# Adding eight gathered expert rows to each token: eight multiply-and-add operations against one wide product, one sum and one addition

## The chip, the cores and the metric

The kernel runs on one core of one Trainium2 chip. The metric is the device time of one execution in microseconds (us); lower is better. The engines of the core are PE (TensorE, the matrix engine; PEld is its weight load), DVE (VectorE), ACT (ScalarE), POOL (GpSimd) and SP (SyncE, which here only issues transfers). A [P, 128] tile holds 128 tokens on 128 partitions and 128 features in the free dimension, float32.

## What is computed

4096 tokens of 128 features pass through two layers, each an attention and a mixture of experts with residual additions:

```
x = x + tanh(g_xattn[0]) * attention0(layernorm(x), ctx)
x = x + tanh(g_ffn[0])   * mixture0(layernorm(x))      # 64 experts, 8 for each token, 2 shared
x = x + tanh(g_xattn[1]) * attention1(layernorm(x), ctx)
x = x + tanh(g_ffn[1])   * mixture1(layernorm(x))      # 8 experts, 2 for each token
```

The part that matters here is the end of mixture0. The router gives each token eight experts with a weight each, `rw`, and

```
routed = einsum('eth,te->th', expert_out, rw)
```

so that eight rows of 128 numbers, each times its token's weight (the gate tanh(g_ffn[0]) is already in it), are added to the token's row of `x`.

## The kernel before

Tokens are held as 32 tiles of 128 (TILES), in two halves of 16 (HTILES); 16 groups of two tiles (GROUPS) go through the attention, each engine running a loop of steps j in which up to six groups are in flight at different stages. There is no scheduler: every engine has its own instruction list, written out by hand, and waits on semaphores. An instruction that waits holds all that stand behind it on its engine.

Mixture0 works by expert. POOL scatters the normalised rows to their experts' places in DRAM (L1794). Then 112 blocks n of work run, 16 for the shared experts and 96 (RTB, index m = n - 16) for the routed ones, four tiles of 128 rows in each. In each block PE turns the rows and multiplies by the gate and up weights (L830), ACT applies the activation (L1092), DVE multiplies the two parts (`hidden`, L1579), PE turns the product and DVE copies it out of PSUM (`copy_hidden`, L1587), PE multiplies by the down weights (L856), ACT copies the results and they are stored to `expert_results` in DRAM (L1100).

The way back is: POOL issues one indirect DMA for each tile t and rank k (`gather`, L1813), which fetches for every token its k-th row; 256 of them in all. They fill a ring: four buffers for the first 16 tiles (`yg`, laid in `xn2T`), seven for the last 16 (`late_rows`, `late_more`). `gathered(t)` gives the buffer, its semaphore and the count at which all eight rows are there. A buffer is fetched into again only when its tile has been combined, which POOL waits for on the semaphore `s_comb` (L1806 and after). The first half's gathers start about when the second half's routed blocks are under way.

DVE combines: `combine_part(t, part)` takes two of the eight ranks, with one SCALAR_TENSOR_TENSOR each (x = rows[:, k] * wk[:, k] + x, L1710), each waiting for the one before through `s_comb`. PIECES is 4. Tiles 0 to 10 (SOONER is 11) are combined in the routed blocks, one part in each block from m = COMBINE_AT[t] = HRTB + 7 + t * 11 // 3 on, after that block's `hidden` and `copy_hidden`. After each pair of tiles `late_stats` (L1684, L1688) takes the next layernorm's statistics at m = COMBINE_AT[2g+1] + PIECES; POOL turns them into 1/deviation (`deviation`, L1835 and L1837) at a fixed place in its list of gathers, and DVE's `late_neg` (L1695) follows at + PIECES + 4.

Tiles 11 to 31 are combined by `combine(t)`, all parts in a row, as the last thing of a step j of the second attention (L1494 and L1517). The steps have one or two tiles: 5, 9, 11, 12 and 13 have two, and so has step 1. The next step of DVE begins with `late_stats` and `max_rows` (L1226), the maximum over the scores; PE's `shift` (L615) waits for it. POOL's list in these steps has up to ten gathers, one `late_deviation` and one `deviation2` (again L1835 and L1837), for which DVE's `norm2_neg` (L1275) waits. Later the gathers are followed by the scatter of the second mixture (L1820).

## Time and profile before

| | before |
|---|---|
| median of 3 runs | 1156.08 us (1152.35 to 1157.39) |
| the profiled execution, its own time | 1156.52 us |
| its span, first to last instruction | 1154.7 us |
| mean granted TensorE clock | 0.881 of 2.4 GHz |
| PE busy | 992.8 us (86%) |
| DVE busy | 749.3 us (65%) |
| POOL busy | 697.1 us (60%) |
| the 256 operations on L1710 | 89.0 us of DVE |

Busy shares are means over stages that have different limits, so the stage has to be looked at: 274 to 664 us are the blocks of mixture0, 664 to 945 us the second attention with the gathers and combines in it, and from there on mixture1. A timeline row has start, duration (us), engine, line, operation, output<-input and shapes; in square brackets the idle time before it and what ended it. "issue" means that nothing in the profile shows a reason.

### The profile page before, as it was taken

The numbers are of one execution on the slowest core, as the hardware profiler recorded it, in microseconds if no ns is written. First come the engines' busy times: TensorE is split into PE (matmuls) and PEld (weight loads), VectorE is DVE, ScalarE is ACT, GpSimd is POOL, SyncE is SP. The second block draws the span as 40 slices with busy tenths as digits, with TensorE's granted clock in tenths as the row PEclk, the third lists the DMA queues.
The fourth block names the chain that finished last, engine by engine and source line by source line (L and its number), as shares of the span: only waits on it lengthen the run. The fifth ranks groups of instructions, "written<-read, shape, count | busy, mean of one in ns | idle before, by whom it ended". The sixth has DMA issues, their size and how long they took to land.

```text
span 1154.7 us, 28212 instructions
## 1 busy us (share of the span) xinstructions
PE 992.8 (86%) x8822; PEld 854.9 (74%) x8822; DVE 749.3 (65%) x2773; ACT 609.9 (53%) x1505; POOL 697.1 (60%) x767
## 2 busy tenths in 40 slices
PE   4888888887997799999999948778889998999991
PEld 2566666665786699999999926666677778999991
DVE  4568888875884378786667635478867644534563
ACT  2566666644332355555555435567564555756660
POOL 1105777776777676006777777777766467765542
PEclk9899999987996799999999965799775667999996
DMA  7434622521246677567777653334222113323434
GB/s 201 99 81 111 165 65 86 154 75 40 70 143 185 187 219 215 168 170 211 221 212 220 185 153 87 91 100 109 57 59 59 41 45 92 91 85 83 139 89 128
DMA packets 228050, 144.03 MB, mean 125 GB/s; under 512 B 55058, under 2 KB 213186, under 8 KB 227906
## 3 DMA queue, kind: packets, MB, share of 16 engines
q1 hardware_dynamic: 151618, 65.37, 21.1%
q0 software_dynamic: 20992, 43.30, 12.4%
q10 hardware_dynamic: 55296, 33.56, 10.2%
q8 instruction: 76, 1.25, 0.5%
q14 instruction: 68, 0.56, 0.2%
HBM read 78.76 MB, written 64.49 MB: 124 GB/s over the span
## 4 chain that ended last, share of the span: by engine, by line
PE 45%; POOL 16%; DVE 14%; issue 9%; DMA 8%; SPq 6%; ACT 3%; DVEq 0%; POOLq 0%; ACTq 0%
PE bank L830 6%; DMA expert_results<-arena 6%; PE bank L856 5%; PE bank L905 4%; PE bank L915 4%; POOL late_more L1813 4%; PE bank L639 3%; PE bank L626 3%; POOL expert_rows L1820 3%; PE bank L807 2%; SPq L487 2%; PE bank L604 2%; PE bank L841 2%; DVE x L1710 2%; PE bank L676 2%
## 5 line engine op out<-in xcount | busy, mean ns | idle before, releaser
L1794 POOL DMA_INDIRECT expert_rows<-xn2T,slot x256 | 252.1, 985 | 95.3 <-issue 72.1
L1813 POOL DMA_INDIRECT xn2T<-expert_results,slot x128 | 124.0, 969 | 102.5 <-DMA expert_results<-arena 64.3
L830 PE MATMUL bank<-wexp,arena 128*128 x768 | 144.9, 334 | 2.3 <-issue 1.1
L986 ACT ACTIVATE work<-bank 128x512 f32<-128x512 f32 x128 | 76.6, 599 | 98.3 <-PE bank L626 95.8
L830 PEld LDWEIGHTS bank<-wexp,arena 128*128 128x128 f32 x768 | 120.2, 197 | 8.2 <-issue 6.4
L1579 DVE TENSOR_TENSOR arena<-arena,bank 128x176 f32<-128x176 f32 x224 | 70.1, 334 | 84.6 <-ACT arena L1092 77.2
L1134 ACT ACTIVATE arena<-bank,wcopy 128x128 f32<-128x128 f32 x320 | 90.8, 370 | 53.9 <-PE bank L905 52.9
L1100 ACT ACTIVATE arena<-bank 128x512 f32<-128x512 f32 x96 | 57.3, 597 | 110.6 <-DMA expert_results<-arena 67.7
L1830 POOL DMA_INDIRECT expert_results<-yb,back x80 | 79.6, 995 | 59.1 <-DVE yb L1732 35.8
L856 PE MATMUL bank<-wexp,arena 88*128 x768 | 107.3, 285 | 5.3 <-ACT arena L1100 4.8
L626 PE MATMUL bank<-cst,work 128*128 128x128 f32 x512 | 98.4, 323 | 14.4 <-DVE arena L1241 7.6
L639 PEld LDWEIGHTS bank<-vm,work 128*64 128x64 f32 x2048 | 83.0, 159 | 30.8 <-ACT work L986 20.0
L856 PEld LDWEIGHTS bank<-wexp,arena 88*128 88x128 f32 x768 | 97.7, 199 | 7.8 <-issue 7.4
L1092 ACT ACTIVATE arena<-bank 128x176 f32<-128x176 f32 x224 | 68.6, 317 | 65.5 <-PE bank L830 33.5
L639 PE MATMUL bank<-vm,work 128*64 128x18 f32 x2048 | 96.2, 230 | 4.4 <-ACT work L986 4.1
L1587 DVE COPY arena<-bank 88x512 f32<-88x512 f32 x112 | 76.6, 684 | 29.9 <-PE bank L841 29.5
L1226 DVE TENSOR_REDUCE nmax<-bank 128x8 fp32r<-128x512 f32 x128 | 85.1, 673 | 16.1 <-PE bank L610 10.8
L990 ACT ACTIVATE work<-bank 128x512 f32<-128x512 f32 x128 | 76.3, 596 | 33.8 <-PE bank L615 33.4
L905 PE MATMUL bank<-xgT,wcopy 128*128 128x128 f32 x640 | 88.8, 283 | 4.6 <-DVE wcopy L1725 4.6
L615 PE MATMUL bank<-nmax,idr 128*128 128x512 f32 x128 | 70.2, 549 | 23.2 <-DVE nmax L1226 23.2
L915 PE MATMUL bank<-wx,arena 128*128 x640 | 85.2, 277 | 0.7 <-ACT arena L1134 0.7
L655 PE MATMUL bank<-arena,wqk 128*128 128x256 f32 x192 | 64.5, 450 | 24.4 <-DVE arena L1241 11.4
(211 smaller groups left out, 2148.0 us busy)
## 6 DMA issues: line engine op xcount, KB each, us to landing
arena<-expert_rows SPq DMA_DIRECT2D x384, 64.0 KB
expert_results<-arena ACTq DMA_DIRECT2D x96, 256.0 KB
expert_rows<-zero SPq DMA_DIRECT2D x130, 64.0 KB
arena<-in_ctxT ACTq DMA_DIRECT2D x32, 256.0 KB
xg<-expert_rows SPq DMA_DIRECT2D x80, 68.0 KB
expert_rows<-xn2T,slot POOLq DMA_INDIRECT x320
wx<-in_mix SPq DMA_DIRECT2D x16, 256.0 KB
late_rows<-expert_results SPq DMA_DIRECT2D x8, 512.0 KB
```

Source lines behind the costliest of these rows:

```text
L626: mm = pe.transpose(w[:, bb * P:(bb + 1) * P], work[:, u, bb * P:(bb + 1) * P], ident)
L639: mm = pe.matmul(w2[b2 * SEQ:(b2 + 1) * SEQ, at:at + 2 * VW], work2[:, u % 2, pair * P + b2 * SEQ:pair * P + (b2 + 1) * SEQ], vm[:, V % 3, ...
L830: mm = pe.matmul(out[:, b * 2 * I0:(b + 1) * 2 * I0], xgT[:, n % 2, 2 * h + b, :], wflat[:, bass.ds(offsets[m][2 * h + b], 2 * I0)], start ...
L856: mm = pe.matmul(bank[7][:, b * P:(b + 1) * P], hT[0:I0, n % 2, b, :], wflat[0:I0, bass.ds(offsets[m][b] + 2 * I0, P)], start=True, stop=T ...
L905: mm = pe.matmul(bank[2 + i % 3][:, c * P:(c + 1) * P], wcopy[:, i % WRING, c * P:(c + 1) * P], xgT1[:, m % 2, i % NB, :], start=True, sto ...
L915: mm = pe.matmul(bank[LATE_Y[m % 2]][:, b * P:(b + 1) * P], hT1[:, i % WRING, c, :], wxflat[:, bass.ds(offsets[m][b] + (W2C + c * P), P)], ...
L986: act.activation(work2[:, u % 2, :], (w0, w3, w3, w3)[u][:, :], ACT.Copy).then_inc(S["pt_copied"], 1)
L1134: a = act.activation(hT1[:, i % WRING, c, :], bank[2 + i % 3][:, c * P:(c + 1) * P], ACT.Gelu_apprx_tanh, bias=wcopy[:, i % WRING, F1 + c: ...
L1226: dve.tensor_reduce(nmax[:, u, :], score[u][:].rearrange("p (a k) -> p a k", k=SEQ), AX.X, ALU.max, negate=True).then_inc(S["max_done"], 1)
L1794: pool.indirect_dma_start(xs, bass.IndirectOffsetOnAxis(ap=slot[:, t, k:k + 1], axis=0), xn2all[:, t, :].bitcast(I32), None).then_inc(s_sc ...
L1813: pool.indirect_dma_start(rows[:, k, :].bitcast(I32), None, ys, bass.IndirectOffsetOnAxis(ap=slot[:, t, k:k + 1], axis=0)).then_inc(ready, 16)
L1830: pool.indirect_dma_start(ys1, bass.IndirectOffsetOnAxis(ap=back[:, i:i + 1], axis=0), yb1[:, m % YR, b, :].bitcast(I32), None).then_inc(s ...
```

## The change

`combine_part` no longer does two ranks in a part. With PIECES = 3, part 0 waits for the eight rows and multiplies all of them in place by the eight weights, one TENSOR_TENSOR over 8 x 128 = 1024 elements for each partition with the weight broadcast along the features; part 1 sums the eight rows with one TENSOR_REDUCE that reads them feature by feature (a step of 128 elements, 512 bytes, within a sum) into one of two 128-element buffers of the first router (`masked` and `rest`); part 2 adds these to the token's row. Each still waits for the one before through `s_comb`, which now counts 3 for a tile, and all waits on it are rescaled. The parts of a tile in the blocks end one block sooner, and `late_stats` and `late_neg` move one block sooner with them.

```diff
-PIECES = 4
+PIECES = 3
@@ the same in every wait on s_comb, one of them shown
-                    pool.wait_ge(s_comb, (t - ring + 1) * TOPK0)
+                    pool.wait_ge(s_comb, (t - ring + 1) * PIECES)
@@ combine_part(t, part)
-                dve.wait_ge(ready, count)
-                if t % HTILES == 0:
+                if part == 0:
+                    dve.wait_ge(ready, count)
+                if part == 0 and t % HTILES == 0:
                     dve.wait_ge(s_norm, 4 * (t // HTILES + 1))
                 xt = x[:, t * P:(t + 1) * P]
-                for k in range(part * 2, part * 2 + 2):
-                    if k:
-                        dve.wait_ge(s_comb, t * TOPK0 + k)
-                    dve.scalar_tensor_tensor(xt, rows[:, k, :], wk[:, t, k:k + 1], xt, ALU.mult, ALU.add).then_inc(s_comb, 1)
+                sums = (masked, rest)[t % 2][:]
+                if part:
+                    dve.wait_ge(s_comb, t * PIECES + part)
+                if part == 0:
+                    a = dve.tensor_tensor(rows, rows, wk[:, t, :].unsqueeze(2).to_broadcast([P, TOPK0, P]), ALU.mult)
+                elif part == 1:
+                    a = dve.tensor_reduce(sums, rows.rearrange("p k d -> p d k"), AX.X, ALU.add)
+                else:
+                    a = dve.tensor_tensor(xt, xt, sums, ALU.add)
+                a.then_inc(s_comb, 1)
```

## Rows read from the trace of the kernel before

**Rows 1.** POOL's lines, 534 to 664 us: busy, mean ns, idle before.
```profile
L1813 POOL DMA_INDIRECT xn2T<-expert_results,slot x98 | 94.3, 962 | 29.4 <-issue 28.4 <-DVE x L1710 0.9
```

**Rows 2.** POOL's timeline: two deviations that waited for DVE.
```profile
658.99 0.22 POOL L1835 TENSOR_SCALAR ve<-mv 128x2 f32<-128x2 f32 x1 [0.86 <-DVE mv L1688]
...
775.63 0.22 POOL L1835 TENSOR_SCALAR ve<-mv 128x2 f32<-128x2 f32 x1 [2.17 <-DVE mv L1268]
```

**Rows 3.** DVE's timeline: norm2_neg in five steps of the second attention.
```profile
732.05 0.16 DVE L1275 SCALAR_TENSOR_TENSOR nm<-mv,rs 128x2 f32<-128x2 f32 x1 [5.80 <-POOL rs L1837]
...
806.11 0.16 DVE L1275 SCALAR_TENSOR_TENSOR nm<-mv,rs 128x2 f32<-128x2 f32 x1 [2.61 <-POOL rs L1837]
...
820.81 0.16 DVE L1275 SCALAR_TENSOR_TENSOR nm<-mv,rs 128x2 f32<-128x2 f32 x1 [2.61 <-POOL rs L1837]
...
837.59 0.16 DVE L1275 SCALAR_TENSOR_TENSOR nm<-mv,rs 128x2 f32<-128x2 f32 x1 [0.58 <-POOL rs L1837]
...
856.34 0.16 DVE L1275 SCALAR_TENSOR_TENSOR nm<-mv,rs 128x2 f32<-128x2 f32 x1 [0.58 <-POOL rs L1837]
```

**Rows 4.** DVE's timeline: two of the steps that combine two tiles.
```profile
859.77 6.43 DVE L1710 SCALAR_TENSOR_TENSOR x<-late_rows,wk,x 128x128 f32<-128x128 f32 x16
...
898.69 6.45 DVE L1710 SCALAR_TENSOR_TENSOR x<-late_more,wk,x 128x128 f32<-128x128 f32 x16
```

**Rows 5.** PE's timeline: the first shift after two such pairs.
```profile
887.12 0.79 PE L615 MATMUL bank<-nmax,idr 128*128 128x512 f32 x1
...
906.58 0.48 PE L615 MATMUL bank<-nmax,idr 128*128 128x512 f32 x1 [2.50 <-DVE nmax L1226]
```

**Rows 6.** DVE by line and shape: busy us, mean ns, idle before.
```profile
L1710 DVE SCALAR_TENSOR_TENSOR x<-xn2T,wk,x 128x128 f32<-128x128 f32 x128 | 44.2, 349 | 3.8
...
L1622 DVE TENSOR_TENSOR junk<-junk,wst 128x512 f32<-128x512 f32 x32 | 22.2, 692 | 1.1
L1624 DVE TENSOR_REDUCE wk<-junk 128x8 f32<-128x512 f32 x32 | 22.0, 686 | 1.1
...
L1327 DVE TENSOR_REDUCE rank<-cmp 128x16 f32<-128x128 f32 x32 | 9.2, 286 | 1.1
...
L1363 DVE TENSOR_REDUCE masks<-masks 128x64 bf16<-128x192 bf16 x14 | 4.9, 347 | 0.0
...
L1603 DVE TENSOR_TENSOR work<-work,key 128x1024 f32<-128x1024 f32 x2 | 2.5, 1225 | 0.1
...
L1189 DVE TENSOR_TENSOR row_f<-row_f,row_part 128x128 f32<-128x128 f32 x4 | 1.2, 294 | 0.1
```

**Rows 7.** POOL's timeline: three indirect DMAs longer than their kind.
```profile
334.04 1.49 POOL L1794 DMA_INDIRECT expert_rows<-xn2T,slot  x1 [0.30 <-issue]
...
346.01 1.45 POOL L1794 DMA_INDIRECT expert_rows<-xn2T,slot  x1 [0.30 <-issue]
...
530.25 2.33 POOL L1813 DMA_INDIRECT xn2T<-expert_results,slot  x1 [0.30 <-issue]
```

**Rows 8.** DVE's timeline at the same three places.
```profile
334.01 0.68 DVE L1619 TENSOR_TENSOR junk<-key,top8p 128x512 f32<-128x512 f32 x1
...
345.93 0.69 DVE L1622 TENSOR_TENSOR junk<-junk,wst 128x512 f32<-128x512 f32 x1
...
530.56 1.21 DVE L1600 SCALAR_TENSOR_TENSOR work<-key,shift_row 128x1024 f32<-128x1024 f32 x1
```

**Rows 9.** POOL's timeline in the step with tile 21.
```profile
794.19 0.94 POOL L1813 DMA_INDIRECT late_more<-expert_results,slot  x1 [0.30 <-issue]
795.44 0.95 POOL L1813 DMA_INDIRECT late_more<-expert_results,slot  x1 [0.30 <-issue]
```

**Rows 10.** DVE's timeline in the same step, its combine.
```profile
794.15 3.30 DVE L1710 SCALAR_TENSOR_TENSOR x<-late_rows,wk,x 128x128 f32<-128x128 f32 x8
```

**Rows 11.** DVE's timeline in a routed block: hidden, after the last combine.
```profile
642.93 0.82 DVE L1579 TENSOR_TENSOR arena<-arena,bank 128x176 f32<-128x176 f32 x2 [0.80 <-ACT arena L1092]
```

**Rows 12.** Windows: PE, PEld, DVE, ACT, POOL busy (x), PEclk, DMA share, GB/s.
```profile
870.00:875.00 5.00, 5.00 (x44) 4.17 (x44) 2.95 (x14) 2.81 (x6) 3.50 (x5) 0.50 0.16 39
```

More of the change, by code:

```diff
@@ L476, in load_late_rows @@
                 if m == 0:
-                    sp.wait_ge(s_comb, TILES * TOPK0)
+                    sp.wait_ge(s_comb, TILES * PIECES)
                 if m >= XR:
@@ L1018, in norm2_apply @@
                         if L and B == 0:
-                            act.wait_ge(s_comb, HTILES * TOPK0)
+                            act.wait_ge(s_comb, HTILES * PIECES)
                         for t in range(2):
@@ L1681, in late_stats @@
                 S = layers[1]
-                dve.wait_ge(s_comb, (g + 1) * 2 * TOPK0)
+                dve.wait_ge(s_comb, (g + 1) * 2 * PIECES)
                 for t in range(2 * g, 2 * g + 2):
@@ L1808, in gather @@
                 if k == 0 and t - h * HTILES >= ring:
-                    pool.wait_ge(s_comb, (t - ring + 1) * TOPK0)
+                    pool.wait_ge(s_comb, (t - ring + 1) * PIECES)
                 elif k == 0 and t - HTILES >= LATE_RING - 4:
-                    pool.wait_ge(s_comb, (t - LATE_RING + 1) * TOPK0)
+                    pool.wait_ge(s_comb, (t - LATE_RING + 1) * PIECES)
                 rows, ready, _ = gathered(t)
@@ L1826, in send_back @@
                 if m == 0:
-                    pool.wait_ge(s_comb, TILES * TOPK0)
+                    pool.wait_ge(s_comb, TILES * PIECES)
                 for b in range(NB):
```

## The prediction

> **What bounds the kernel now.** I read the page first: in its first part (the table above has it) DVE is busy for 65% and POOL for 60% of the span, so neither is the limit of the whole, and 89 us of DVE time in the combine says little by itself. The combine lies between 540 and 905 us, and there I read the chain of work that ended last, then the waits of DVE, PE and POOL. They show three stretches.
>
> In the routed blocks (540 to 664 us) PE sets the pace of the blocks and DVE waits for ACT in each of them; the shortest such wait while a tile is combined is 0.80 us [rows 11]. But POOL runs beside it without a gap: 98 indirect DMAs in 130 us, and nearly all idle time before them is the 0.30 us between one and the next that no other engine causes [rows 1]. One starts every 1.25 us [rows 9]. POOL stopped only once for a result, 0.86 us for the statistics [rows 2].
>
> From 664 to 820 us POOL is what the steps of the second attention wait for. DVE's norm2_neg stands idle 5.80 us for POOL's deviation at 732 us, and 2.61 us at 806 and 820 us [rows 3]: the deviation stands in POOL's list behind the gathers. A microsecond more in POOL's list between 534 and 820 us is therefore a microsecond more on the end, though not every step: the one at 763 us has two tiles to combine and there DVE is last, POOL waits 2.17 us for it at 775 us [rows 2].
>
> From 820 to 905 us the steps with two tiles wait for DVE: the pair takes 6.43 us [rows 4], max_rows stands behind it, and PE's shift waits 2.50 us after the pair at 898 us [rows 5]. The pair at 879 us is different: its shift follows at 887.12 with no idle time [rows 5], PE had work until then. So four pairs are on the path, at 763, 823, 859 and 898 us; the single tiles are not.
>
> **Part by part: DVE's time for one tile.** Removed: eight operations of 0.349 us [rows 6], each waiting for the one before. A pair of tiles, 16 of them, takes 6.43 us from first start to last end [rows 4], so 0.40 each with the gaps, 3.2 us for a tile. Added: the product, 1024 elements with both inputs in SBUF; the nearest rows are 1.225 us for the same size and 0.692 for half of it. I take 1.21, as an operation with one input broadcast has [rows 8]. The sum over eight rows: the same kind of operation on 512 elements takes 0.686 us, as much as a product of 512 (0.692), so 1.22 for 1024. The final addition: 0.29 us [rows 6]. With gaps of 0.04 us that is 2.8 us for a tile, and 5.5 for a pair, where the second product overlaps the end of the first addition. A pair on the path gains 0.93 us; four gain 3.7. At 763 us POOL comes next, after the 2.17 us, of which the hold below takes 1.3, so about 0.85 is left there: 3.6 us in all.
>
> The unknown in this is the step of 512 bytes with which the sum reads. The one reduction in the trace that reads across takes a step of 128 bytes (bfloat16): 192 elements in 0.347 us [rows 6]. A line through the reductions of 128 elements (0.286 us) and 512 (0.686) gives 0.353. So the step cost nothing there. Bounds: 1.22 us, and with each element at twice its time (0.15 fixed, 1.07 for the elements) 2.3 us. I take 1.22, since 0.347 is the row nearest in kind. The Trainium skill (Advanced Engine Details and Errata, Memory Cachelines) says that SBUF is read in lines of 16 bytes and that a pattern which meets another line at each access pays for it; by that rule the sum would lie towards the upper bound, which is a rival below. By that rule the 0.347 us would be longer too, and they are not.
>
> In the routed blocks the first two parts are 0.5 us longer than the two operations they replace (0.72 us), inside the 0.80 us of idle time [rows 11]; the third is shorter. Twice (after tiles 3 and 9) late_stats, 0.75 us, now falls into the block that begins another tile's product, together 1.2 us more than now, 0.4 beyond the idle time. PE has a block's work in hand, so I take 0; without that cover it is 0.8 us for both. The ring's buffers come free one block (3 us) sooner, which POOL waited for by 0.9 us in three waits at most [rows 1]; those are the usual 0.30 us between two DMAs, so nothing is gained. The statistics also come 3 us sooner: the 0.86 us at 659 us [rows 2] go, -0.9.
>
> **Part by part: what the wide product does to POOL.** This is the part that decides. An indirect DMA on POOL takes 0.95 us. The one at 334.04 took 1.49 us: DVE's TENSOR_TENSOR of 512 elements had begun at 334.01 and ended at 334.69. The one at 346.01 took 1.45 us: that DVE operation ended at 346.62. The one at 530.25 took 2.33 us: behind DVE's running copy stood the 1024-element operation of 530.56, which ended at 531.77 [rows 7, 8]. In each case the extra time is what DVE had left, less 0.12 us (0.53, 0.49, 1.39). An indirect DMA that begins after the DVE operation has begun is held to its end; one that begins a little before is not, unless the DVE operation already stands queued behind another, as at 530.25. The Trainium skill (SBUF — State Buffer, Who interferes with whom) says that two SBUF inputs of DVE lock out GpSimd's reads for the whole instruction, but infers that tensor_tensor leaves the generation of descriptors alone. By that inference there would be no hold, and the sum would be the second rival's. The three rows speak against it.
>
> The small operations hold little: 0.35 us less 0.12 leaves 0.23 at most, and in the blocks the mean is 0.962 us against 0.944 undisturbed, 98 x 0.018 = 1.8 us [rows 1], of which 0.6 is the first DMA after each deviation. So 1.2 us for 11 tiles. A product of 1.21 us meets a DMA nearly always, as one starts each 1.25 us. With phases at random the mean hold is 1.09 x 1.09 / 2 / 1.25 = 0.475 us. Walking a queue of this pitch past the recorded starts of the first operation of tiles 0 to 16 gives less, 0.36 to 0.40 a tile, 6.2 us for the 17 until 745 us. Less 1.2 and 0.2 for the old holds: +4.8.
>
> After that DVE and POOL start together from the deviation, and the phase is fixed. In the step with tile 21 the combine begins at 794.15 and a DMA at 794.19 [rows 9, 10]: a product from 794.15 to 795.36 has 1.17 us left then, less 0.12 a hold of 1.05 us. Tiles 20 and 22 have the same phase to 0.01 us. 3 x 1.05 = 3.2, if the product takes the exact place of the first small operation; if it begins 0.05 us later the DMA is ahead and nothing is held, so this term lies between 0 and 3.2. The 0.02 us seen now stands for the small ones. Behind 830 us POOL has 1 us or more to spare in each step, and holds cost nothing.
>
> **The sum.** On the profiled execution, 1156.5 us (span 1154.7 and 1.8 around it; 0.4 above the median): pairs -3.6; statistics -0.9; holds until 745 us +4.8; fixed phases +3.2. That is +3.5, 1160.0 us, and 1159.6 from the median. I take 1160. The terms' own bounds: random holds of 0.475 each (+1.9) and 0.8 for the blocks make it 1162.7; the fixed phases at nothing 1157.
>
> **The rivals.** (1) The reading across is dear. If the sum takes 2.3 us, a tile costs 3.9 us instead of 3.2, and each of the four pairs loses 1.3 instead of gaining 0.93: +8.9 against my sum, 1169, slower than before. It decides from 1.65 us for the reduction on, where a tile costs what it did. For it: the step is four times the one in the trace. Against it: that row shows no trace of a price. (2) POOL is not held, or not where it counts: then only the gains remain, 1156.5 - 3.6 - 0.9 = 1152. For it: the small operations from 794.15 on held nothing [rows 9, 10]. Against it: [rows 7, 8]. (3) The clock. PE is at 0.50 of full speed in stretches such as 870 to 875 us [rows 12], after the gap behind a pair, and a step takes 18.75 us there (837.59 to 856.34) against 14.70 at full speed (806.11 to 820.81) [rows 3]. Steps 6 to 8 grow by 1 us in which PE is idle; if the clock falls there two steps at the low level cost 8 us: 1168. The other way, pairs 0.9 us shorter could spare one of the three falls: 1152 or less. The gap at 906 us was 2.5 us and the clock fell, so shortening seems not enough. (4) The product is no faster for DVE than eight operations: the rows of 1.2 us exclude it.
>
> **How the numbers follow.** My forecast has 0.45, with a range of its own of 1156 to 1164; rival 2, or only half the holds, 0.25 (1151 to 1156); the clock to the worse 0.13 (1164 to 1171); the dear reading 0.08 (1166 to 1173); the clock to the better 0.07 (below 1151); the rest 0.02. The range 1151 to 1168 leaves out the last two and the far end of the clock. A measurement of this kernel can tell about 0.5%, 5.8 us, so the border is at 1161.9 and 1150.3. Slower: 0.25 of my own case, and the two dear ones: 0.11 + 0.13 + 0.08 = 0.32. Faster 0.10, same 0.58.
>
> **What would show it.** The new lines: a product of 1.21 us, a sum of 1.22, an addition of 0.29; a sum above 1.65 is rival 1. POOL's L1813 in 534 to 664 us with a mean near 1.00 us instead of 0.962, and single DMAs near 2.0 us at each product in the steps at 780 to 810 us. The last gather of tile 15 later by 3 us or so. The wait of PE's first shift behind a pair 0.9 us shorter. If the means of L1813 don't move, the hold is wrong; if they do and norm2_neg's waits don't move with them, POOL was not the bound I take it for. A stretch of low clock between 775 and 815 us, or one less after 820, would move the time by more than all of this.

## The result and the profile after

The changed kernel takes 1167.3 us (median of 4 runs, 1162.65 to 1171.12), the kernel before 1154.21 beside it (1144.37 to 1157.39): ratio 1.0131, 95% interval 1.0094 to 1.0168. It is slower: by 13 us between the medians, by 15 by the ratio. The forecast was 1160; 1167.3 lies in the range of 1151 to 1168, close to its upper end. The profiled execution took 1171.12 us, span 1169.3, against 1156.52 and 1154.7.

First VectorE (DVE) by line and shape, after; the columns behind the bar are busy us, mean ns and idle time before.

```profile
L1712 DVE TENSOR_TENSOR xn2T<-xn2T,wk 128x1024 f32<-128x1024 f32 x16 | 19.4, 1213 | 0.0
L1714 DVE TENSOR_REDUCE masked<-xn2T 128x128 f32<-128x1024 f32 x8 | 15.6, 1952 | 0.1
...
L1714 DVE TENSOR_REDUCE rest<-late_rows 128x128 f32<-128x1024 f32 x4 | 7.6, 1903 | 0.1
L1716 DVE TENSOR_TENSOR x<-x,masked 128x128 f32<-128x128 f32 x16 | 4.7, 291 | 0.3
```

The product is 1.21 us as foretold and the addition 0.29, but the sum is 1.90 to 1.95 us where I had 1.22. A tile now takes 3.5 us instead of the 3.26 to 3.30 of before [rows 10].

Then POOL's lines from 534 to 664 us, after. This answers [rows 1].

```profile
L1820 POOL DMA_INDIRECT xn2T<-expert_results,slot x92 | 97.0, 1054 | 27.6 <-issue 27.6
```

The mean went from 962 to 1054 ns where I had expected near 1000, so that 92 gathers fit where 98 did. Single ones show how. POOL's and DVE's timelines at 611 us, and at 845 us:

```profile
611.13 2.53 POOL L1820 DMA_INDIRECT xn2T<-expert_results,slot  x1 [0.31 <-issue]
...
845.07 2.00 POOL L1820 DMA_INDIRECT late_rows<-expert_results,slot  x1 [0.30 <-issue]
```

```profile
611.02 0.69 DVE L1587 COPY arena<-bank 88x512 f32<-88x512 f32 x1 [0.18 <-PE bank L841]
611.63 1.21 DVE L1712 TENSOR_TENSOR xn2T<-xn2T,wk 128x1024 f32<-128x1024 f32 x1
...
845.03 1.22 DVE L1712 TENSOR_TENSOR late_more<-late_more,wk 128x1024 f32<-128x1024 f32 x1
846.28 1.90 DVE L1714 TENSOR_REDUCE rest<-late_more 128x128 f32<-128x1024 f32 x1
848.22 0.29 DVE L1716 TENSOR_TENSOR x<-x,rest 128x128 f32<-128x128 f32 x1
```

At 845.07 the DMA begins 0.04 us into a product, and it takes 2.00 us instead of 0.944: 1.06 more, which is the 1.18 that the product had left, less 0.12. At 611.13 the product had not begun; it stood queued behind a copy, and the DMA was held for all of it: 1.59 us more. 28 gathers took over 1.10 us, against 2 before. What stands queued decides. Over all traces of this document 24 DMAs of POOL began during a copy out of PSUM with a product, a multiply-and-add or a copy of 1024 elements queued next, and all 24 were held to that operation's end; 214 began so with a product of 512 elements next, and none was held beyond the copy's end; and 47 with a reduction next, of which none was held. The copy alone holds nothing: in the changed kernel 20 DMAs began in one (L1587, 0.68 us) at least 0.27 us before its end with no such operation behind, and the longest was lengthened by 0.03 us.

What it does to the path: DVE's norm2_neg after, which answers [rows 3]. In the kernel before these six steps stood at 732.05, 747.22, 760.92, 776.69, 806.11 and 911.97 us.

```profile
745.01 0.16 DVE L1275 SCALAR_TENSOR_TENSOR nm<-mv,rs 128x2 f32<-128x2 f32 x1 [17.65 <-POOL rs L1844]
760.36 0.16 DVE L1275 SCALAR_TENSOR_TENSOR nm<-mv,rs 128x2 f32<-128x2 f32 x1 [0.58 <-POOL rs L1844]
778.86 0.16 DVE L1275 SCALAR_TENSOR_TENSOR nm<-mv,rs 128x2 f32<-128x2 f32 x1 [0.58 <-POOL rs L1844]
796.07 0.16 DVE L1275 SCALAR_TENSOR_TENSOR nm<-mv,rs 128x2 f32<-128x2 f32 x1 [0.58 <-POOL rs L1844]
...
826.51 0.16 DVE L1275 SCALAR_TENSOR_TENSOR nm<-mv,rs 128x2 f32<-128x2 f32 x1 [2.21 <-POOL rs L1844]
...
931.23 0.16 DVE L1275 SCALAR_TENSOR_TENSOR nm<-mv,rs 128x2 f32<-128x2 f32 x1 [0.58 <-POOL rs L1844]
```

The step of 732 us stands at 745: 13.0 us late, and DVE waited 17.65 us for POOL. And TensorE in the windows that follow (PE busy, granted clock, DMA share, GB/s):

```profile
732.00:745.00 13.00, 0.00 (x0) 0.50 0.19 50
745.00:760.00 15.00, 14.29 (x111) 0.50 0.35 97
760.00:775.00 15.00, 15.00 (x118) 0.50 0.33 90
```

PE stood idle for all 13 us, and then worked for 30 us at 0.50, its lower level of 1.2 GHz, where the kernel before had a mean of 0.82 over 732 to 775 us. The steps got 5.0 us later still in it (760.92 became 778.86, 17.9 late).

The product held deviations too. The deviation of 598 us began ahead of a product that ran from 598.69 to 599.90, and it took 1.44 us instead of 0.24, to 0.08 us behind the product's end:

```profile
598.54 1.44 POOL L1842 TENSOR_SCALAR ve<-mv 128x2 f32<-128x2 f32 x1
```

The account of the 14.6 us of span, up to 745 us: first gather 1.1 us later; holds of gathers +11.0 (their time over 0.944 us is 14.7 us in 155 gathers, 3.7 before); the deviations between them +1.8 (1.2 at 598 us and 0.7 at 717 us, where it took 0.92 us; the others took 0.1 less in all); less 0.9 for the statistics that POOL no longer waits for. That is all of the 13.0. Then the stretch at low clock, +5.0. Behind it the lateness goes up and down, 21.5 us at 821 us, 17.4 at 860, 19.3 at 912. After that 5.0 us come back at once and 2.3 more by 980: PE's clock is 0.83 in 910 to 945 us where it was 0.59. The last 2.6 us arise in the second mixture; what makes them stays open.

The first shift behind a pair answers [rows 5]:

```profile
905.37 0.80 PE L615 MATMUL bank<-nmax,idr 128*128 128x512 f32 x1 [0.42 <-DVE nmax L1226]
...
925.27 0.50 PE L615 MATMUL bank<-nmax,idr 128*128 128x512 f32 x1 [3.12 <-DVE nmax L1226]
```

The second waits 3.12 us instead of 2.50: longer by 0.6, where I had said shorter by 0.9. The pair is now the slower one.

### The profile page after: what moved, and what is told of

Same layout as the page of the kernel before. It is cut to its first block, busy times and chain, and to the rows that moved or that the text cites. A ratio compares the mean times of both kernels' runs of the same rounds, so it can differ in the third digit from the quotient of the medians.

```text
span 1169.3 us, 27956 instructions
## 1 busy us (share of the span) xinstructions
PE 981.8 (84%) x8822; PEld 846.6 (72%) x8822; DVE 768.5 (66%) x2613; ACT 610.4 (52%) x1505; POOL 724.1 (62%) x767
## 3 DMA queue, kind: packets, MB, share of 16 engines
q0 software_dynamic: 20992, 43.30, 12.2%
## 4 chain that ended last, share of the span: by engine, by line
PE 41%; POOL 22%; DVE 15%; issue 10%; SPq 5%; ACT 3%; DMA 3%; DVEq 0%; POOLq 0%; ACTq 0%
POOL xn2T L1820 12%; PE bank L905 5%; PE bank L915 5%; PE bank L830 4%; PE bank L626 3%; PE bank L639 3%; PE bank L856 3%; POOL late_more L1820 3%; SPq L487 2%; PE bank L604 2%; POOL expert_rows L1827 2%; PE bank L676 2%; PE bank L807 2%; PE bank L841 2%; POOL expert_rows L1801 2%
## 5 line engine op out<-in xcount | busy, mean ns | idle before, releaser
L1820 POOL DMA_INDIRECT xn2T<-expert_results,slot x128 | 135.0, 1055 | 101.1 <-DMA expert_results<-arena 62.9
L830 PE MATMUL bank<-wexp,arena 128*128 x768 | 141.2, 327 | 2.9 <-issue 1.7
L830 PEld LDWEIGHTS bank<-wexp,arena 128*128 128x128 f32 x768 | 116.8, 193 | 8.2 <-issue 6.5
L1587 DVE COPY arena<-bank 88x512 f32<-88x512 f32 x112 | 76.6, 684 | 33.1 <-PE bank L841 26.4
L626 PEld LDWEIGHTS bank<-cst,work 128*128 128x128 f32 x512 | 63.8, 159 | 37.4 <-issue 34.1
L905 PEld LDWEIGHTS bank<-xgT,wcopy 128*128 128x128 f32 x640 | 80.8, 198 | 8.1 <-DVE wcopy L1732 8.0
```

The source lines that it names most:

```text
L626: mm = pe.transpose(w[:, bb * P:(bb + 1) * P], work[:, u, bb * P:(bb + 1) * P], ident)
L830: mm = pe.matmul(out[:, b * 2 * I0:(b + 1) * 2 * I0], xgT[:, n % 2, 2 * h + b, :], wflat[:, bass.ds(offsets[m][2 * h + b], 2 * I0)], start ...
L905: mm = pe.matmul(bank[2 + i % 3][:, c * P:(c + 1) * P], wcopy[:, i % WRING, c * P:(c + 1) * P], xgT1[:, m % 2, i % NB, :], start=True, sto ...
L1587: dve.tensor_copy(hT[0:I0, n % 2, :, :].rearrange("p b n -> p (b n)"), bank[6][0:I0, :]).then_inc(b_htc, 1)
L1820: pool.indirect_dma_start(rows[:, k, :].bitcast(I32), None, ys, bass.IndirectOffsetOnAxis(ap=slot[:, t, k:k + 1], axis=0)).then_inc(ready, 16)
```

## The experiments

**The sum, the product's hold, and both: e1, e2, e3.** Theory A was: holds and slow sum each cost, the holds most. Theory B: the sum alone. Theory C: the clock, whatever the two do. One line of the changed kernel each:

```diff
 e1 -  a = dve.tensor_reduce(sums, rows.rearrange("p k d -> p d k"), AX.X, ALU.add)
    +  a = dve.tensor_reduce(sums, rows.rearrange("p k d -> p (k d)").rearrange("p (d k) -> p d k", k=TOPK0), AX.X, ALU.add)
 e2 -  a = dve.tensor_tensor(rows, rows, wk[:, t, :].unsqueeze(2).to_broadcast([P, TOPK0, P]), ALU.mult)
    +  a = dve.tensor_reduce(wsel[:, 0:TOPK0], rows, AX.X, ALU.add)
 e3    both
```

> The changed kernel with one line altered: the sum reads eight adjacent elements for each result instead of eight elements that lie 512 bytes apart (so it adds the wrong elements; number of elements, result and everything else stay). Every theory expects the sum at 1.2 us instead of 1.92 if the distance between the elements is its price, and at 1.92 if it is not. Theory A (the product's holds on POOL's DMA instructions cost most, the slow sum the rest): the holds stay at a mean of 0.8 us a tile, the second layer's mean-times-rstd step near 760 to 780 us stays 10 us or more late, and the four pairs of tiles give back 4 x 2 x 0.7 = 5.6 us, so the ratio to the kernel before falls from 1.013 to about 1.008. Theory B (the slow sum alone makes the loss, POOL's holds are covered): the ratio falls to 1.000 or below. Theory C (the loss is the clock's, whatever the two do): the ratio stays at 1.013 within 0.003.

> The changed kernel with the wide product replaced by an addition over the same 1024 elements, which reads one tensor instead of two (the weights are not applied, so the rows are added unweighted). Its time on VectorE should be 1.2 us as the product's. Theory A: a VectorE operation that reads one tensor holds no DMA instruction of POOL, so the gathers return to 0.95 us each, the late step near 760 to 780 us comes back to within 3 us of its time before, and of the loss of 15 us some 11 go: ratio about 1.003, what stays being the slow sum's. Theory B (slow sum alone): nothing moves, ratio 1.013. Theory C (clock alone): the ratio follows no rule, and the shift ahead of the first stretch at half clock (732 us) stays at 13 us.

> Both edits of the two runs before it in one kernel: no operation that reads two tensors over 1024 elements, and a sum over adjacent elements (neither weights nor the right rows in the sum). It leaves what I had forecast for VectorE alone: a tile at 2.8 us, four pairs at 0.93 us less than before and statistics 0.9 us earlier, 4 to 5 us of gain with no hold on POOL. Theory A: ratio 0.996 to 0.998, and the two single edits' gains add up to this one's. Theory B: the same as the run with the adjacent sum alone. Theory C (clock alone): no better than 1.008.

| | ratio to before (95%) | sum, us | gathers over 0.944 us in all | norm2_neg of 732 us | span |
|---|---|---|---|---|---|
| changed | 1.0131 (1.0094 to 1.0168) | 1.92 | 28.4 | +13.0 | 1169.3 |
| e1 | 1.0069 (1.0040 to 1.0099) | 1.21 | 24.8 | +9.9 | 1166.5 |
| e2 | 0.9972 (0.9943 to 1.0002) | 1.92 | 5.7 | -1.7 | 1145.0 |
| e3 | 0.9898 (0.9857 to 0.9939) | 1.21 | 5.4 | -2.8 | 1141.7 |
| before | 1 | | 6.8 | 0 | 1154.7 |

The sum's step is worth 0.0062 (7 us), the product's hold 0.0159 (18 us), both together 0.0233; the single ones add up to 0.0221. By the intervals each of these differences is good to about 0.005. (The profiled execution of e1 was 7 us above its median, so its span is not to be compared.) B and C fall: e2 leaves DVE's time as it was and the loss is gone. The size was above what A said (1.003). In its profile PE is not left idle at 732 us, and its clock is up. TensorE's windows in e2 (the same columns):

```profile
732.00:745.00 13.00, 10.25 (x137) 1.00 0.38 108
745.00:760.00 15.00, 12.53 (x177) 1.00 0.41 119
760.00:775.00 15.00, 10.74 (x108) 0.73 0.28 76
```

and its norm2_neg:

```profile
730.32 0.16 DVE L1275 SCALAR_TENSOR_TENSOR nm<-mv,rs 128x2 f32<-128x2 f32 x1 [3.74 <-POOL rs L1844]
743.92 0.16 DVE L1275 SCALAR_TENSOR_TENSOR nm<-mv,rs 128x2 f32<-128x2 f32 x1 [3.42 <-POOL rs L1844]
757.54 0.16 DVE L1275 SCALAR_TENSOR_TENSOR nm<-mv,rs 128x2 f32<-128x2 f32 x1 [2.36 <-POOL rs L1844]
```

A step takes 13.6 us here; after, in the low stretch, 18.5 (760.36 to 778.86). Between the two profiles norm2_neg is 14.7 us apart in the first step, and 4.9 more arise in the low stretch. I read the first as POOL's and the second as the clock's, brought on by POOL's lateness; no run changes the clock by itself. That e2 is not above the kernel before (its interval reaches 1.0002), with a tile 0.25 us longer, goes with a higher clock all the way (0.81, 0.76 and 0.84 in 820:870, 870:910 and 910:945, where before had 0.66, 0.59, 0.59); why PE's clock came out so is open.

**Two chains instead of one: e4.** Eight operations stay; they go by turns into x and into a spare tile (the first into the spare tile only multiplies), and a ninth adds the two. COMB is 9.

```diff
-  if k:
-      dve.wait_ge(s_comb, t * TOPK0 + k)
-  dve.scalar_tensor_tensor(xt, rows[:, k, :], wk[:, t, k:k + 1], xt, ALU.mult, ALU.add)
+  into = (xt, sums)[k % 2]
+  if k > 1:
+      dve.wait_ge(s_comb, t * COMB + k - 1)
+  if k == 1:
+      a = dve.tensor_scalar(into, rows[:, k, :], wk[:, t, k:k + 1], None, ALU.mult)
+  else:
+      a = dve.scalar_tensor_tensor(into, rows[:, k, :], wk[:, t, k:k + 1], into, ALU.mult, ALU.add)
...
+  if part == 3:
+      dve.wait_ge(s_comb, t * COMB + 8)
+      dve.tensor_tensor(xt, xt, sums, ALU.add)
```

> The kernel before, with its eight multiply-and-add operations dealt out to two accumulators, even ranks into x and odd ranks into a spare tile, so that each waits for the one before the last and not for the last, and one addition of the two at the end. No work is left out. If what the old chain costs is each operation's wait for the result before it (eight at 0.35 to 0.41 us), a tile takes about 8 x 0.29 + 0.29 = 2.6 us instead of 3.26, and there is no operation of 1024 elements that reads two tensors. Theory A (holds of the wide product plus the slow sum made the loss): 4 pairs x 2 x 0.6 = 5 us gained, ratio 0.995, unless operations of 128 elements lying close behind one another hold POOL's instructions as one long one does; then the ratio is 1.000 or above. Theory B (VectorE's time alone counts): 0.995. Theory C (clock alone): anything within 0.3 per cent of 1.

Measured: ratio 0.9943 (0.9913 to 0.9973), 1146.19 us against 1153.02: the best kernel here that does the whole work, 1.9% below the changed one. DVE's timeline of a tile in it:

```profile
862.60 0.35 DVE L1716 SCALAR_TENSOR_TENSOR masked<-late_rows,wk,masked 128x128 f32<-128x128 f32 x1
862.86 0.35 DVE L1716 SCALAR_TENSOR_TENSOR x<-late_rows,wk,x 128x128 f32<-128x128 f32 x1
863.12 0.34 DVE L1716 SCALAR_TENSOR_TENSOR masked<-late_rows,wk,masked 128x128 f32<-128x128 f32 x1
863.39 0.34 DVE L1716 SCALAR_TENSOR_TENSOR x<-late_rows,wk,x 128x128 f32<-128x128 f32 x1
```

One begins each 0.26 us though it lasts 0.35: what made the old chain 0.40 was the wait for the result before. A tile takes 2.45 to 2.5 us instead of 3.26 to 3.30, and the holds stay small: 7.6 us in all, 6.8 before. Operations of 128 elements close behind one another do not lock POOL out as one long one does. Nor did they in the kernel before: 67 gathers began during one of its 256 operations, and none was lengthened by over 0.13 us.

**Where the sum's price begins: e8.** The step between the elements goes by the tile.

```diff
-  a = dve.tensor_reduce(sums, rows.rearrange("p k d -> p d k"), AX.X, ALU.add)
+  step = 1 << (t // 2 % 8)
+  a = dve.tensor_reduce(sums.rearrange("p (a s) -> p a s", s=step), rows.rearrange("p k d -> p (k d)").rearrange("p (a k s) -> p a s k", k=TOPK0, s=step), AX.X, ALU.add)
```

> The changed kernel with the sum's reading step set by the tile: each of its eight elements lies 1, 2, 4, 8, 16, 32, 64 or 128 elements of 4 bytes from the next, every two tiles another step, 128 x 1024 elements each time (all but the last step add the wrong elements). One look for the durations. If the price belongs to a step that leaves some small block of the buffer, the time goes from 1.21 us to 1.9 at one step between 4 and 64 bytes and stays there; if it belongs to long steps, it rises gradually up to 512 bytes. The whole should lie between the kernel before and the changed one plus nothing: about 1160 us.

DVE's timeline: tiles 2 and 3 (8 bytes), then tile 4 (16 bytes).

```profile
707.85 1.20 DVE L1715 TENSOR_REDUCE masked<-xn2T 128x128 f32<-128x1024 f32 x1
736.22 1.21 DVE L1715 TENSOR_REDUCE rest<-xn2T 128x128 f32<-128x1024 f32 x1
745.38 1.98 DVE L1715 TENSOR_REDUCE masked<-xn2T 128x128 f32<-128x1024 f32 x1
```

| step, bytes | 4 | 8 | 16 | 32 | 64 | 128 | 256 | 512 |
|---|---|---|---|---|---|---|---|---|
| sum, us (four tiles) | 1.21 to 1.22 | 1.20 to 1.22 | 1.97 to 2.00 | 1.99 to 2.01 | 1.87 to 1.90 | 1.87 to 1.95 | 1.90 to 1.93 | 1.90 to 1.95 |

It is a threshold between 8 and 16 bytes, not a slope: 0.7 us more on 1024 elements, 0.7 ns for each, and no more at 512 bytes than at 16. The Trainium skill (Advanced Engine Details and Errata, Memory Cachelines) says that SBUF is read in lines of 16 bytes and that reading a new line at each access costs; this run agrees with it, threshold and all. The 1160 us that I gave for the whole can't be compared: this run fell on a chip where the kernel before takes 1472 us (see below) and took 1457.

**The product in two halves: f1.**

```diff
-  a = dve.tensor_tensor(rows, rows, wk[:, t, :].unsqueeze(2).to_broadcast([P, TOPK0, P]), ALU.mult)
+  for k in range(0, TOPK0, 4):
+      a = dve.tensor_tensor(rows[:, k:k + 4, :], rows[:, k:k + 4, :], wk[:, t, k:k + 4].unsqueeze(2).to_broadcast([P, 4, P]), ALU.mult)
```

> The changed kernel with the product cut into two of four rows. Theory A: where the kernel before takes about 1153 us, no hold over 0.6 us, holds of 10 us in all beyond the kernel before instead of 22, ratio about 1.006. Theory B (VectorE's time alone): 1.014. On a slow chip (kernel before near 1480 us) 1.000 to 1.004 by either, which tells nothing.

Ratio 1.0063 (1.0031 to 1.0094), as A has it. Gathers over 0.944 us come to 16.0 in all (28.4 with one product). The longest hold by a half was 0.64 us, of a gather that began 0.15 us before the end of the first half and was held by the second too; the others were 0.55 at most. DVE and POOL at one of them:

```profile
558.66 1.28 DVE L1714 TENSOR_TENSOR xn2T<-xn2T,wk 128x512 f32<-128x512 f32 x2
```

```profile
557.70 0.94 POOL L1825 DMA_INDIRECT xn2T<-expert_results,slot  x1 [0.30 <-issue]
558.95 1.21 POOL L1825 DMA_INDIRECT xn2T<-expert_results,slot  x1 [0.30 <-issue]
```

The DMA of 558.95 begins in the first half, which ends at 559.34, and is held 0.27 us, that half's 0.39 less 0.12; the second half does not hold it. norm2_neg of 732 us stands at 731.6, though here the first gather of all came 3.9 us sooner, so that 3.5 of lateness are in it, against 11.9 in the changed kernel. VectorE's time even rose, since two halves take 1.28 us where one product takes 1.21; theory B fails here a second time. (This kernel too has one gather held by the operation that holds at 530.25 in [rows 7, 8], 1.58 us here.)

**Product and sum each added to the kernel before: f2, f3.** Behind the eighth operation of each tile one more whose result is unused:

```diff
 f2 +  dve.tensor_tensor(rows, rows, wk[:, t, :].unsqueeze(2).to_broadcast([P, TOPK0, P]), ALU.mult)
 f3 +  dve.tensor_reduce(wsel[:, 0:TOPK0], rows, AX.X, ALU.add)
```

> The kernel before with an unused wide product of 1.22 us behind each tile's eighth operation. Theory A: ratio 1.018 to 1.022 where the kernel before takes about 1153 us, and the mean-times-rstd step of 732 us in the kernel before 11 to 15 us late. Theory B: the ratio of the next run.

> The kernel before with an unused addition over one tensor's 1024 elements, 1.22 us too, behind each tile's eighth operation. Theory A: ratio 1.007 to 1.010, the step of 732 us at most 2 us late. Theory B: the same ratio as the run with the product. On the slow chip this run gave 1.013 and the product's 1.016.

f2: 1.0197 (1.0152 to 1.0242), f3: 1.0154 (1.0113 to 1.0195), both operations 1.22 us. The product holds POOL by 8.3 us more in all (14.4 against 6.1), and its ratio is 0.0043 higher, 5.0 us; but the intervals overlap, and the difference is below the 0.008 I had set, so this pair doesn't decide against B; e2 and f1 do. Nor is norm2_neg of 732 us late by 11 to 15: it stands at 734.2, 5.3 later than its first gather would have it, because the product stands behind eight operations here and met 18 gathers by over 0.16 us where the changed kernel's met 28. What misses is f3: no hold, norm2_neg of 732 us at 732.93 (0.9 late), as said, but then it loses more than four pairs could: DVE's timeline,

```profile
732.93 0.16 DVE L1276 SCALAR_TENSOR_TENSOR nm<-mv,rs 128x2 f32<-128x2 f32 x1 [2.56 <-POOL rs L1841]
746.66 0.16 DVE L1276 SCALAR_TENSOR_TENSOR nm<-mv,rs 128x2 f32<-128x2 f32 x1 [2.79 <-POOL rs L1841]
762.43 0.16 DVE L1276 SCALAR_TENSOR_TENSOR nm<-mv,rs 128x2 f32<-128x2 f32 x1 [0.58 <-POOL rs L1841]
783.23 0.16 DVE L1276 SCALAR_TENSOR_TENSOR nm<-mv,rs 128x2 f32<-128x2 f32 x1 [0.58 <-POOL rs L1841]
```

and the step of 912 us in the kernel before is 22.4 us late. That is 21.5 us in between, for 16 tiles of 1.22 us each, 19.5 us. But they do not come tile by tile. The five steps with a pair of tiles bring 17.5 us, for 12.2 of added time; the six single tiles bring 4.1, for 7.3. And 5.0 us come in one pair's step, from 762.43 to 783.23 us, where PE's clock is low (the columns as above):

```profile
760.00:775.00 15.00, 15.00 (x122) 0.50 0.25 65
775.00:790.00 15.00, 13.42 (x107) 0.50 0.26 71
```

The kernel before had 0.89 and 1.00 in these windows. So VectorE's time is on the path mostly in the pairs, as foretold, in all five and not in four, and some of the loss is the clock's; how much, no run separates.

**On another chip: e5, e6, e7, e9 to e12.** These runs fell on two chips where the kernel before takes 1472 (e5 to e7) and 1494 us (e9 to e12), not 1153. e5 to e7 and e10 to e12 are the kernels of f1, f2 and f3 (halves, product added, reduction added), e9 is the changed kernel.

> The changed kernel itself, on the same chip as the three runs beside it, since the chip of the run with the halves gave 1472 us for the kernel before and not 1153, with other phases in which far fewer gathers met a product. On a chip where the kernel before takes 1153 us: ratio 1.013, holds of 22 us in all. On the slower chip: fewer gathers meet a product, and Theory A (holds plus slow sum) expects 1.003 to 1.008 there.

| beside the kernel before on its chip | ratio (95%) |
|---|---|
| e9, changed | 1.0002 (0.9973 to 1.0031) |
| e5 and e10, halves | 1.0012 (0.9974 to 1.0049), 1.0038 (1.0013 to 1.0064) |
| e6 and e11, product added | 1.0152 (1.0082 to 1.0221), 1.0161 (1.0117 to 1.0205) |
| e7 and e12, reduction added | 1.0123 (1.0008 to 1.0237), 1.0132 (1.0101 to 1.0163) |

> The changed kernel with its wide product cut into two of four rows each, issued one behind the other, the same work in all; sum and addition as they were. Theory A (an instruction of POOL that issues a DMA during an operation that reads two tensors is held until shortly before that operation's end, and then goes): no hold is longer than 0.6 us instead of 1.15, a gather that falls into the pair of halves is let through between them, so the hold per tile falls to a half or less, 6 to 9 of the loss of 15 us go in spite of 0.05 to 0.1 us more VectorE time a tile, and the ratio to the kernel before is about 1.006. Rival (two operations back to back hold POOL as one long one): the longest holds stay at 1.1 us and the ratio at 1.013 to 1.015.

> The kernel before, with its eight operations, and behind each tile's eighth one more: the wide product of the changed kernel, whose result nobody uses. Theory A: it costs 1.2 us of VectorE a tile (four pairs: about 10 us late in the second layer) and as many holds as in the changed kernel (12 to 14 us at 745 us): ratio 1.015 to 1.022. Theory B (only VectorE's time counts): the same as the next run, whose added operation has the same length: about 1.009.

> The kernel before, with its eight operations, and behind each tile's eighth one more of the same 1.2 us: an addition over 1024 adjacent elements, one tensor read, whose result nobody uses. Theory A: VectorE's time alone, no hold: the mean-times-rstd step at 732 us in the kernel before is late by under 2 us, then 1 to 2.5 us more for each of four pairs: ratio 1.004 to 1.010, and 0.008 or more below the run with the product added. Theory B: the same ratio as that run's.

> The changed kernel with the product cut into two of four rows, as before, here for its time beside that of the changed kernel on the same chip. On the slower chip a gather that met the first half was let through between the halves and no hold was over 0.41 us. Theory A: 0.005 to 0.008 below the changed kernel where the kernel before takes 1153 us (about 1.006), 0.002 to 0.004 below it on the slower chip. Theory B (VectorE's time alone counts; a tile is 0.15 us longer with two halves): equal to the changed kernel or 0.001 above.

> The kernel before with the unused product behind each tile's eighth operation. Where the kernel before takes 1153 us, Theory A expects 1.018 to 1.022: 10 us from 1.2 us more VectorE time a tile in the pairs, 11 to 15 us from holds. Theory B: as the run with the added reduction.

> The kernel before with the unused addition over 1024 elements, of one tensor and of the same length, behind each tile's eighth operation. Where the kernel before takes 1153 us, Theory A expects 1.007 to 1.010 and at least 0.008 below the run with the product. Theory B: the same ratio as that run, both near 1.009.

There the same change costs nothing, against my 1.003 to 1.008. The halves are 0.0036 above it, where A had said 0.002 to 0.004 below. The two added operations cost 1.2 to 1.6%, the product 0.003 more than the reduction, which is within the intervals and short of the 0.008 of A. The shares by engine of the chain that ended last, in e9 and then after:

```profile
PE 46%; another core or an unknown queue 17%; DVE 14%; issue 9%; ACT 6%; SPq 4%; DMA 4%; POOL 0%; DVEq 0%; POOLq 0%; ACTq 0%
```

```profile
PE 41%; POOL 22%; DVE 15%; issue 10%; SPq 5%; ACT 3%; DMA 3%; DVEq 0%; POOLq 0%; ACTq 0%
```

And POOL's waits from 653 to 900 us in e9, the time of the gathers there:

```profile
POOL ve L1842 <- DVE mv L1688: 69.6, 5, 20.9
```

POOL waits 69.6 us in five waits for statistics, since the blocks are slow there (ACT waits up to 28.2 us for a queue that the profile doesn't name). The product still holds it (e9's gathers have 15.4 us over 0.944, and 15 took over 1.10 us), but into time that it would have waited. The hold is a fact of the operation; its price is one of the path. This reading rests on one profile of each kernel. What slows the blocks on those chips wasn't pursued.

**Which operations hold POOL: f4, g1.** Another wide operation in the product's place, changing every two tiles; the sum stays. The rows are weighted as they should be only where the product stands.

```diff
 f4 +  tensor_tensor as it is; tensor_scalar(rows, rows, wk[:, t, 0:1]); scalar_tensor_tensor(rows, rows, 1.0, wide); tensor_copy(rows, rows)
 g1 +  tensor_reduce(rows, rows.unsqueeze(3)); tensor_scalar(turned, turned, wk[:, t, 0:1]); tensor_copy(turned, turned)
       # turned = rows.rearrange("p k d -> p d k")
```

> The changed kernel in which the wide operation in the product's place goes by the tile, two tiles each: the product of two tensors as it is; a multiplication by one weight for each partition (one tensor read); a scaled product of two tensors in one operation; a plain copy (one tensor read). The sum stands behind each. One look: if what holds POOL is that two tensors are read, DMA instructions that start during the first and third kind are lengthened to 0.12 us before its end and none during the second and fourth; if what holds is a wide operation that writes 1024 elements (the unweighted addition writes only 8), they are lengthened in all four.

> The changed kernel with another wide operation in the product's place, by the tile, two tiles each: an addition over one element each (it reads and writes all 1024); a multiplication by one weight and a copy that both read and write with a step of 512 bytes (one tensor read, 1024 written). The sum stands behind each. One look. If writing 1024 elements is what holds, DMA instructions of POOL that start during any of the three are lengthened to 0.12 us before its end. If it is two tensors read or double speed, none is lengthened during an operation that takes 1.1 us or more, and one that still takes 0.7 us holds.

f4, POOL and DVE, a plain copy of 1024 elements:

```profile
818.66 1.47 POOL L1828 DMA_INDIRECT late_more<-expert_results,slot  x1 [0.30 <-issue]
```

```profile
818.62 0.69 DVE L1720 COPY late_rows<-late_rows 128x1024 f32<-128x1024 f32 x1
```

The DMA is held 0.53 us, to the copy's end less 0.12. All four kinds did this, with 26 of the 27 DMAs that began during one of them; the one left began 0.01 us behind its copy. g1, DVE and POOL, a reduction that writes 1024 elements at 698 us, and a copy across at 820 us:

```profile
698.08 1.21 DVE L1714 TENSOR_REDUCE xn2T<-xn2T 128x1024 f32<-128x1024 f32 x1
...
820.73 1.31 DVE L1718 COPY late_rows<-late_rows 128x1024 f32<-128x1024 f32 x1
```

```profile
698.37 0.94 POOL L1826 DMA_INDIRECT xn2T<-expert_results,slot  x1 [0.30 <-issue]
...
820.77 2.07 POOL L1826 DMA_INDIRECT late_more<-expert_results,slot  x1 [0.30 <-issue]
```

The reduction held none of the 10 DMAs that began in it, though it writes 1024 elements: "what writes 1024 elements holds" falls. The copy across takes 1.31 us and holds, 1.13 us, which my other rule had forbidden for anything over 1.1 us; so did the multiplication across, 1.37 us long, by up to 1.04 us. It may be the fast copy (0.69) paying 0.62 us for its 512-byte step, nearly the 0.7 of the sum, so "two tensors read, or double speed" is not refuted, but not shown either. What is shown is which operations held: tensor_tensor, scalar_tensor_tensor, tensor_scalar and copy did, with 512 or 1024 elements read from SBUF; tensor_reduce never, nor the reciprocal of 128 elements (0.95 us, 83 DMAs in all traces), nor the copies out of PSUM.

The Trainium skill (SBUF — State Buffer, Who interferes with whom) says that tensor_reduce never contends with GpSimd, that copy and tensor_scalar do in their two-port modes, and that two SBUF inputs block only GpSimd's reads, from which it infers that tensor_tensor leaves descriptor generation alone. The first two agree with these runs as far as they go, since no run shows the mode of an operation; the inference does not: 1.06 us of hold on the DMA at 845.07.

## Why the prediction failed, step by step

**The product's time: right.** 1.213 to 1.218 us for a forecast of 1.21, and 0.29 for the addition.

**The sum's time: wrong, the first of the two steps that failed.** I took 1.22 us because a reduction of 192 bfloat16 elements with a step of 128 bytes showed no price [rows 6]. It took 1.92, past the 1.65 from which rival 1 decides. e8 shows the price at every step from 16 bytes on in float32. Why the bfloat16 row shows none wasn't tried. The rule of 16 bytes, quoted beside it from the Trainium skill (Advanced Engine Details and Errata, Memory Cachelines), was the better guide here; one row of another type and a fifth of the size was too little to set it aside at a chance of 0.08. The pairs then lose some 0.5 us each instead of gaining 0.93: instead of -3.6 about +2, an estimate; e1 gives 7 us to the sum in the whole.

**The hold: right in kind, half in size.** The rule read from three rows [rows 7, 8] holds to within 0.01 us in all but two of the product's holds (0.03 and 0.04 there): end of the DVE operation, less 0.12, less the DMA's start. The second step that failed is the size in the random phases: 0.36 to 0.40 a tile, 6.2 us for 17 tiles. In the trace after 16 products ran ahead of 745 us; 13 of them held a gather, by 0.91 us on average, 11.8 us in all, and two more held a deviation, 1.9 us, a term that the sum doesn't have. Three of these holds (1.59, 1.15 and 1.22 us) are longer than a product can give to a DMA that begins in it; there the product stood queued behind another operation as the DMA began. I had read that very case at 530.25 and left it out of the walk. For the rest, I walked along recorded starts, and these move with the change. The fixed phases came as said: 1.05 to 1.06 us where a DMA begins 0.04 behind the product (829.3, 845.07, 877.2 and 897.1 us), but of tiles 20 to 22 only tile 22 had it; the three held for 2.0 us instead of 3.2.

**Which steps pay for DVE: right in the main, not settled.** I let four pairs pay, not the one at 879 us. In f3 all five do, and the single tiles a little. That DVE can be last behind a single tile stands in the trace of before: POOL waited 2.32 us for DVE's statistics ahead of norm2_neg at 856 us, whose own idle time of 0.58 us [rows 3] is the way from these statistics over POOL and back.

```profile
855.28 0.22 POOL L1835 TENSOR_SCALAR ve<-mv 128x2 f32<-128x2 f32 x1 [2.32 <-DVE mv L1268]
```

But that step, 837.59 to 856.34, is also the one at PE's low clock that takes 18.75 us against 14.70 [rows 3], so f3 doesn't give each tile's price. e3 is what I had forecast for DVE without the hold; it came to 0.9898, 10 to 12 us of gain where my terms gave 4.5. Before 821 us it is only 0.3 us ahead in norm2_neg, and the rest comes behind, where its clock is 0.76 against 0.50 in 835 to 850 us. Again the clock and DVE's time are not separated.

**The clock.** Rival 3 had the mechanism but in the wrong place. PE starved for 13 us ahead of 745 and then ran at half clock for 30 us, in which the steps lost 5.0 us; later stretches ran at a higher clock than before (0.93 against 0.66 in 820 to 870 us) and gave some back. I had looked for it only behind 775 us.

**Together.** The forecast of +3.5 was the sum of -4.5 from DVE and +8.0 from holds. What came: from DVE a loss instead of a gain, since the sum takes 1.92 us and not 1.22; by 745 us holds of 11.0 on gathers and 1.8 on deviations instead of 4.8; and their echo in the clock. That 1167.3 still lies in the range is luck: the range was open on that side for rivals 1 and 3, and rival 3's stretch was looked for in another place. Rival 1's time, 1169, is nearly what was measured, but by less than half through its mechanism: e1 gives the sum's step 7 us, e2 the hold 18, together more than the loss of 15, since e3, without both, is faster than the kernel before.

## What to carry to other kernels

When GpSimd issues a dense row of indirect DMAs on the path, every VectorE operation tried on 512 or 1024 elements in SBUF, but the reduction, holds the DMA that meets it until 0.12 us before its end (some that began in its first 0.04 us were let through). So wide operations can cost more than eight of 128 that take longer in sum: e1's tile takes 2.8 us of VectorE, the old one 3.3, and e1 is 0.7% slower. Fold over the axis that lies adjacent, or at most 8 bytes apart; a sum across rows cost 0.7 ns more for each element. And where small operations form a chain, look at the pitch against the duration (0.40 against 0.26): two accumulators removed the wait, did the same work, and beat both kernels.

## What the hardware showed that I had not expected

- The price of a float32 reduction's step is all or nothing: 1.2 us for 1024 elements at 4 and 8 bytes, 1.87 to 2.01 from 16 to 512.
- A DMA instruction of POOL waits even for a DVE operation of 1024 elements that has not begun but stands queued: 1.59 us at 611.13, and 24 times of 24 behind a copy out of PSUM. For a product of 512 elements queued there it never did, 0 of 214.
- A plain copy from SBUF to SBUF, one tensor in and 0.69 us long, holds POOL as the product does, and a copy out of PSUM of the same length does not; a reduction that reads and writes 1024 elements in 1.21 us does not.
- The same change is 1.3% slower on one chip and 1.0002 on another, with the program unchanged; by the profile, POOL has waits on the second that cover the holds.
